# Softmax attention stage: full-width side products split into four strips of 32 output columns

## The chip, the cores and the metric

One program on one core of a Trainium2 chip. The metric is the device time of one execution in microseconds, as the median of several runs. Besides its time, one execution of the kernel was recorded by the hardware profiler; everything that is said of durations comes from that record.

## What is computed

The reference is a chain of six layers on `x` of shape (4, 1024, 128) in fp32. The part in which the change lies is the softmax attention, 16 heads of 8 channels, together with the second channel-mixing layer, which is computed beside it:

```python
x = x + 0.5 * _L0_ffn_ref(_layernorm(x), L0_ffn_W_r, L0_ffn_W_k, L0_ffn_W_v, L0_ffn_mu_r, L0_ffn_mu_k)
x = x + _L0_attn_ref(_layernorm(x), L0_attn_qkv_w, L0_attn_qkv_b, L0_attn_proj_w, L0_attn_proj_b)
x = x + 0.5 * _L0_ffn_ref(_layernorm(x), ...)        # the same weights a second time
x = x + 0.5 * _L1_ffn_ref(...)                       # 8 experts, top 2
x = x + _L1_attn_ref(...)                            # linear attention
x = x + 0.5 * _L1_ffn_ref(...)

def _L0_attn_ref(x, qkv_w, qkv_b, proj_w, proj_b):
    q, k, v = split_heads(x @ qkv_w.T + qkv_b)       # 16 heads of 8
    q, k = apply_rotary(q), apply_rotary(k)
    attn = softmax(q @ k^T * 8 ** -0.5)              # 1024 x 1024 for each head
    return (attn @ v) @ proj_w.T + proj_b

def _L0_ffn_ref(x, W_r, W_k, W_v, mu_r, mu_k):
    xr, xk = mix(x, x_prev, mu_r), mix(x, x_prev, mu_k)
    return sigmoid(xr @ W_r.T) * (relu(xk @ W_k.T) ** 2 @ W_v.T)
```

## The kernel before

The token axis is cut into 32 tiles of 128 tokens, four tiles make a group (512 tokens, one PSUM bank), two groups a batch. The program has stages that follow one another: a start (the first channel mixing of the first groups and the queries and keys of batch 0), the softmax attention, expert loops, the linear attention, expert loops again.

The attention stage is a list of 256 steps (`A_STEPS`: 4 batches, 2 halves of queries, 4 groups of four heads, 8 tiles of keys). TensorE runs, in program order and for each step n (function `pe_attention`):

- the scores (L986): four bf16 matmuls of 50 contracted rows by 128 output columns, moving 512 elements each, two at rows 0 to 49 and two at rows 64 to 113 of the array, into two of three pairs of PSUM banks. Each pair waits until the exponentials of three pairs earlier are done;
- the side pieces that a planner (`plan_attention`) put on this step: at most one of those that use TensorE;
- the weighted sums of step n - 2 (L1003): four fp32 matmuls, each with 128 contracted rows and 18 output columns and 512 moving elements. The four go to PSUM partitions 0, 32, 64 and 96, so each takes one strip of 32 array columns. They wait for the exponentials of their step.

An fp32 matmul stands as two records in the trace. So L986 has four records a step and L1003 eight. ScalarE runs two exponentials of 128x1024 for each step (L1275, `attn_probs<-ps`).

The side pieces are the rest of the work of this stage: the queries, keys and values of the next batch, the division and projection of the finished heads, and the second channel mixing, whose layer is spread over the stage. All of them go through one PSUM bank (`AUX`, bank 7), so a piece waits until VectorE or ScalarE has read out the one before it. Those that use TensorE are:

- `rot` (L890): a rotated or unrotated half of queries or keys, one fp32 product of 128x128 weights with 256 moving elements;
- `norms` (L900): one bf16 product with 512 moving elements;
- `val` (L912): the values, two fp32 products with 128 moving elements a piece;
- `proj` (L948): the projection, four fp32 products with 128 moving elements;
- `mk` (L769): one fp32 product with 512 moving elements; `mr` (L773) and `mv` (L779): four fp32 products with 128 moving elements each;
- transposes (L595, helper `pe_turn_group`), the router's products (L1457) and some small ones (L921, L930).

VectorE and GpSimd work for the same pieces: `dve_attention_side` and `dve_side_mix` take the products out of PSUM (L1099 for `rot`, L1129 for `norms`), split queries and keys into bf16 parts (L1106 to L1125), divide (L1152, L1156) and normalise (L584). Each engine takes the pieces of a step in the same order, which is written out in `k.a_plan`.

## Time and profile before

| | us |
|---|---|
| three runs, median (lowest to highest) | 1315.74 (1309.18 to 1320.01) |
| span of the profiled execution, first to last instruction | 1294.8 |
| difference of the median and the span | 20.9 |
| the attention stage within the span, first to last exponential | 84.0 to 647 |

The profiled execution has no time of its own beside its span, so the difference of 20.9 us between the median of the runs and the span stands for what lies around the span. In the trace, PE is TensorE's matmuls and PEld its weight loads, DVE is VectorE, ACT ScalarE, POOL GpSimd. A matmul's row gives its start and its full duration, which reaches beyond the start of the next one, since matmuls are pipelined: the pitch from start to start is what counts for the time. "idle before" is how long the engine had nothing to do before the instruction, and the arrow names what released it.

### The profile page before, as it was taken

What the parts mean: (1) busy time and instruction counts of PE and PEld (TensorE: products, weight loads), DVE (VectorE), ACT (ScalarE), POOL (GpSimd) and SP (SyncE); (2) the same over time, 40 slices, a digit from 0 to 9 for tenths busy, and PEclk for the clock granted to TensorE, in tenths of its full rate; (3) what the DMA queues carried; (4) which work ended last, traced back from release to release, by engine and by line L of the source; (5) the groups of instructions that cost most, each with busy time, mean ns of one, the idle gap of its engine ahead of it and who ended that gap; (6) DMA issues with size and microseconds to landing.
All of it is one profiled execution on the core that took longest, in us unless ns stands there. A gap on an engine that the chain in (4) does not pass through costs nothing. (4 is left out here: it accounts for less than half of the span.)

```text
span 1294.8 us, 21020 instructions
## 1 busy us (share of the span) xinstructions
PE 1070.8 (83%) x7616; PEld 500.4 (39%) x7616; DVE 653.5 (50%) x2099; ACT 807.3 (62%) x1164; POOL 373.6 (29%) x376
## 2 busy tenths in 40 slices
PE   4479998999999999999978858888877986998940
PEld 3242222322222231232256535534544554665620
DVE  5762555366356332333156326657867684633522
ACT  4348787877898989999934525555544441464520
POOL 2100110211110102333010664144331165265435
PEclk8679998999999999999998979989888897998975
DMA  5270370027028500300011323200000011233422
GB/s 144 55 105 1 58 101 2 1 41 106 14 42 120 157 1 15 114 17 18 19 38 49 104 83 94 68 17 20 15 14 5 1 34 58 72 109 110 133 66 67
DMA packets 83796, 74.08 MB, mean 57 GB/s; under 512 B 11440, under 2 KB 77872, under 8 KB 82800
## 3 DMA queue, kind: packets, MB, share of 16 engines
q1 hardware_dynamic: 73900, 54.93, 19.2%
q0 software_dynamic: 8192, 16.79, 4.4%
q8 instruction: 66, 1.08, 0.4%
q10 hardware_dynamic: 1604, 0.99, 0.3%
q14 instruction: 34, 0.28, 0.1%
HBM read 39.26 MB, written 33.42 MB: 56 GB/s over the span
## 5 line engine op out<-in xcount | busy, mean ns | idle before, releaser
L1275 ACT ACTIVATE attn_probs<-ps 128x1024 f32<-128x1024 f32 x512 | 485.5, 1072 | 73.1 <-PE ps L986 73.0
L1003 PE MATMUL ps<-attn_probs,attn_v 128*18 128x512 f32 x2048 | 274.9, 610 | 6.3 <-DVE room L1234 5.6
L1641 POOL DMA_INDIRECT slots<-moe_xr,moe_slot x128 | 124.8, 975 | 184.4 <-ACT attn_probs L1275 82.7
L986 PE MATMUL ps<-stack 50*128 50x512 bf16 x1024 | 166.2, 389 | 7.2 <-issue 1.2
L1651 POOL DMA_INDIRECT moe_back<-results,moe_slot x128 | 123.3, 963 | 115.2 <-PE ps L1696 45.4
L1706 PE MATMUL ps<-stack,lin_scores 128*128 x312 | 153.1, 613 | 0.0
L1807 ACT ACTIVATE lin_scores<-ps 128x256 f32<-128x256 f32 x156 | 58.5, 382 | 114.9 <-PE ps L1706 114.8
L986 PEld LDWEIGHTS ps<-stack 50*128 50x128 bf16 x1024 | 34.0, 94 | 244.1 <-ACT attn_probs L1275 229.3
L1780 DVE TENSOR_TENSOR lin_scores<-ps,lin_scores 128x256 f32<-128x256 f32 x156 | 59.1, 419 | 104.6 <-ACT lin_scores L1807 104.5
L1732 PE MATMUL ps<-stack,lin_scores 128*128 x624 | 85.1, 280 | 4.8 <-ACT lin_heads_out L1820 4.8
L1732 PEld LDWEIGHTS ps<-stack,lin_scores 128*128 128x128 f32 x624 | 77.4, 195 | 6.5 <-issue 6.5
L1706 PEld LDWEIGHTS ps<-stack,lin_scores 128*128 128x128 f32 x312 | 55.5, 199 | 39.5 <-issue 39.5
L1313 POOL TENSOR_TENSOR room<-room 128x512 f32<-128x512 f32 x16 | 22.2, 1387 | 165.2 <-DVE room L1099 165.2
L1003 PEld LDWEIGHTS ps<-attn_probs,attn_v 128*18 128x18 f32 x2048 | 34.8, 96 | 76.8 <-issue 52.8
L1773 DVE TENSOR_SCALAR lin_scores<-ps,c_norm_scale 128x256 f32<-128x256 f32 x80 | 37.9, 474 | 51.1 <-PE ps L1696 50.6
L1696 PE MATMUL ps<-c_ident,moe_gathered 128*128 128x128 f32 x156 | 33.1, 294 | 36.2 <-DMA moe_gathered<-slots 28.7
L2138 DVE TENSOR_TENSOR lin_scores<-ps,c_causal 128x512 f32<-128x512 f32 x64 | 41.1, 683 | 37.1 <-PE ps L2009 37.1
L2208 ACT ACTIVATE lin_scores<-ps 128x512 f32<-128x512 f32 x64 | 34.7, 594 | 37.4 <-PE ps L2009 37.4
L1099 DVE SCALAR_TENSOR_TENSOR room<-ps,c_attn_b,moe_xr 128x512 f32<-128x512 f32 x32 | 23.9, 749 | 65.3 <-PE ps L890 63.8
L1718 PEld LDWEIGHTS ps<-c_ident,lin_scores 128*128 128x128 f32 x312 | 39.0, 143 | 37.4 <-issue 35.0
L1813 ACT ACTIVATE lin_scores<-ps 128x512 f32<-128x512 f32 x80 | 46.7, 584 | 10.1 <-PE ps L1718 7.2
L552 DVE BATCH_NORM_STATS2 stats<-x 128x6 f32<-128x128 f32 x192 | 41.5, 279 | 19.9 <-POOL x L864 8.3
(237 smaller groups left out, 1552.1 us busy)
## 6 DMA issues: line engine op xcount, KB each, us to landing
moe_gathered<-slots SPq DMA_DIRECT2D x76, 128.0 KB, 2.3
results<-lin_heads_out SPq DMA_DIRECT2D x76, 128.0 KB
stack<-qk_parts SPq DMA_DIRECT2D x36, 256.0 KB, 8.9
slots<-zeros SPq DMA_DIRECT2D x2, 2496.0 KB, 15.2
qk_parts<-moe_xr SPq DMA_DIRECT2D x32, 128.0 KB, 2.7
qk_parts<-moe_xr SPq DMA_DIRECT2D x16, 192.0 KB, 2.8
stack<-in_expert_w SPq DMA_DIRECT2D x1, 3072.0 KB, 10.4
stack<-qk_parts SPq DMA_DIRECT2D x12, 192.0 KB, 10.6
```

The source lines that it names most:

```text
L552: instruction = V.bn_stats(out=k.stats[:, t, :], in_=k.x[:, t, :])
L986: instruction = T.matmul(k.ps[:, SCORE_BANKS[i % 3][s], :], d.stack[b % 2][rows, 1, pair, kt * P:(kt + 1) * P], d.stack[b % 2][rows, 0, pa ...
L1003: instruction = T.matmul(k.ps[32 * j:32 * j + STRIP, PV_BANK, :], d.v[:, b % 2, kt, first:first + STRIP], d.probs[:, n % A_PROBS, j * BANK ...
L1275: A.activation(d.probs[:, n % A_PROBS, 2 * e * BANK:2 * (e + 1) * BANK], k.ps[:, banks[0]:banks[1] + 1, :].rearrange("p a n -> p (a n)"), ...
L1641: G.indirect_dma_start(out=k.dram["slots"][half], out_offset=bass.IndirectOffsetOnAxis(ap=d.slot[:, s, at, c:c + 1], axis=0), in_=d.xr[:, ...
L1651: G.indirect_dma_start(out=k.back[:, at % RING, c, :], out_offset=None, in_=k.dram["results"][half], in_offset=bass.IndirectOffsetOnAxis(a ...
L1706: T.matmul(k.ps[:, bank, :], d.gt[:, u % NB, i, :], w[:, bass.ds(offset[u, i], 2 * HIDDEN)], start=True, stop=True).then_inc(k.full[bank], 1)
L1732: instruction = T.matmul(k.ps[:, bank, i * DIM:(i + 1) * DIM], d.ht[:, u % NB, i, c * P:(c + 1) * P], w[:, 2 * HIDDEN + c * DIM:][:, bass. ...
L1780: V.tensor_tensor(d.h[:, u % NB, i, :], k.ps[:, bank, 0:HIDDEN], d.silu[:, u % NB, i, :], ALU.mult).then_inc(k.free[bank], 1)
L1807: A.activation(d.silu[:, u % NB, i, :], k.ps[:, bank, HIDDEN:2 * HIDDEN], ACT_FN.Silu).then_inc(k.e_silu, 1)
L1813: A.activation(d.ht[:, u % NB, 0:width, :].rearrange("p i c -> p (i c)"), k.ps[:, bank, 0:width * HIDDEN], ACT_FN.Copy).then_inc(k.free[ba ...
L2138: V.tensor_tensor(d.scores[:, m % NS, :].rearrange("p (j t) -> p j t", j=HPG), k.ps[:, bank, :].rearrange("p (j t) -> p j t", j=HPG), caus ...
```

## The change

A helper `pe_product` writes one product of 128x128 weights as several matmuls, each with a share of the output columns. With `strips=4` it makes four matmuls of 32 output columns, at PSUM partitions 0, 32, 64 and 96, each with the whole contraction of 128 rows and the same moving operand. With `strips=1` it makes the matmul of before. Only the attention stage passes `HPG`, which is 4; the start and the expert loops keep one strip. Transposes, L1457, L921 and L930 stay as they are. The semaphore is raised by the last strip.

```diff
+def pe_product(T, out, weights, moving, strips):
+
+    width = P // strips
+    for j in range(strips):
+        cols = slice(width * j, width * (j + 1))
+        instruction = T.matmul(out[cols, :], weights[:, cols], moving, start=True, stop=True)
+    return instruction
+
+
-def pe_side_mix(T, k):
+def pe_side_mix(T, k, strips=1):
...
-            T.matmul(k.ps[:, bank, :], w[:, 1, :], d.mixed_k, start=True, stop=True).then_inc(k.full[bank], 1)
+            pe_product(T, k.ps[:, bank, :], w[:, 1, :], d.mixed_k, strips).then_inc(k.full[bank], 1)
...
-                instruction = T.matmul(k.ps[:, bank, i * P:(i + 1) * P], d.mixed_r[:, i * P:(i + 1) * P], w[:, 0, :],
-                                       start=True, stop=True)
+                instruction = pe_product(T, k.ps[:, bank, i * P:(i + 1) * P], d.mixed_r[:, i * P:(i + 1) * P], w[:, 0, :], strips)
...
-            instruction = T.matmul(k.ps[:, bank, cols], w[:, 2 * qk + which, :],
-                                   d.xt[:, half * BANK:(half + 1) * BANK][:, cols], start=True, stop=True)
+            instruction = pe_product(T, k.ps[:, bank, cols], w[:, 2 * qk + which, :],
+                                     d.xt[:, half * BANK:(half + 1) * BANK][:, cols], strips)
...
 def pe_attention(T, k):
     d = k.attn
-    side = pe_attention_side(T, k)
+    side = pe_attention_side(T, k, HPG)
...
-    mix, route = pe_side_mix(T, k), pe_route(T, k)
+    mix, route = pe_side_mix(T, k, HPG), pe_route(T, k)
```

`mv`, `norms`, `val` and `proj` are edited in the same way. Counted in the programs, the pieces that the change reaches in the attention stage are 48 `rot`, 12 `norms`, 12 `val`, 7 `proj` and 11 each of `mk`, `mr` and `mv`: 112 in all. The order of VectorE, ScalarE, GpSimd and the DMA queues is the same before and after.

TensorE's order around a `rot` piece, in the middle of batch 0's steps, before (`room` holds the transposed input, `c_qk_w` the weights; 128x256 is the output):

```order
L986 MATMUL ps<-stack 128x512 x4
L890 MATMUL ps<-room,c_qk_w 128x256
L1003 MATMUL ps<-attn_probs,attn_v 18x512 x4
L986 MATMUL ps<-stack 128x512 x4
L900 MATMUL ps<-room,same_head_bf 128x512
```

and after:

```order
L993 MATMUL ps<-stack 128x512 x4
L756 MATMUL ps<-room,c_qk_w 32x256 x4
L1010 MATMUL ps<-attn_probs,attn_v 18x512 x4
L993 MATMUL ps<-stack 128x512 x4
L756 MATMUL ps<-room,same_head_bf 32x512 x4
```

Nothing changes its place; the one matmul has become four of 32 output columns (all at the helper's line, L756), still between the scores and the weighted sums.

The same around the products of four tiles, `mr` and `proj`, some 15 steps later, before:

```order
L773 MATMUL ps<-c_mix_w,mix_mixed_r 128x128 x4
L1003 MATMUL ps<-attn_probs,attn_v 18x512 x4
L986 MATMUL ps<-stack 128x512 x4
L595 MATMUL ps<-c_ident,room 128x128 x4
...
L948 MATMUL ps<-c_attn_vo,room 128x128 x4
L1003 MATMUL ps<-attn_probs,attn_v 18x512 x4
```

and after:

```order
L756 MATMUL ps<-c_mix_w,mix_mixed_r 32x128 x16
L1010 MATMUL ps<-attn_probs,attn_v 18x512 x4
L993 MATMUL ps<-stack 128x512 x4
L595 MATMUL ps<-c_ident,room 128x128 x4
...
L756 MATMUL ps<-c_attn_vo,room 32x128 x16
L1010 MATMUL ps<-attn_probs,attn_v 18x512 x4
```

Four matmuls have become sixteen, that is eight records sixteen times two; the transposes (L595) are as before.

## Rows read from the trace of the kernel before

**Rows 1.** Windows of the attention stage, exponentials (L1275) alone: window, length, busy (count), clock

```profile
84.00:470.00 386.00, 319.62 (x334) 0.96 0.32 56
470.00:647.00 177.00, 165.86 (x179) 1.00 0.10 34
```

**Rows 2.** Waits in the attention stage: who for whom, us in total, times, longest

```profile
ACT attn_probs L1275 <- PE ps L986: 73.0, 136, 5.3
```

**Rows 3.** Timeline of PE, two steps without a side piece: start, duration, what

```profile
519.71 0.92 PE L986 MATMUL ps<-stack 50*128 50x512 bf16 x4
...
521.54 0.92 PE L986 MATMUL ps<-stack 50*128 50x512 bf16 x4
```

**Rows 4.** Timeline of PE, steps with a `rot` piece

```profile
344.77 0.60 PE L986 MATMUL ps<-stack 50*128 50x512 bf16 x4
345.30 0.70 PE L890 MATMUL ps<-room,c_qk_w 128*128 128x256 f32 x2
345.93 1.05 PE L1003 MATMUL ps<-attn_probs,attn_v 128*18 128x512 f32 x8
346.92 0.60 PE L986 MATMUL ps<-stack 50*128 50x512 bf16 x4
```

**Rows 5.** Timeline of PE, steps with `mk` and `mr`

```profile
609.84 1.13 PE L769 MATMUL ps<-room,c_mix_w 128*128 128x512 f32 x2
610.89 1.05 PE L1003 MATMUL ps<-attn_probs,attn_v 128*18 128x512 f32 x8
...
612.41 1.16 PE L773 MATMUL ps<-c_mix_w,mix_mixed_r 128*128 128x128 f32 x8
613.50 1.05 PE L1003 MATMUL ps<-attn_probs,attn_v 128*18 128x512 f32 x8
```

**Rows 6.** Timeline of PE, end of the stage: weighted sums of two steps running on

```profile
644.59 1.91 PE L1003 MATMUL ps<-attn_probs,attn_v 128*18 128x512 f32 x16
```

**Rows 7.** Timeline of PE, linear attention: short strips running on

```profile
1073.16 0.84 PE L2022 MATMUL ps<-lin_scores,lin_v 128*9 128x128 f32 x24
1073.82 0.25 PE L1952 MATMUL ps<-lin_v,lin_k_tok 128*32 128x36 f32 x8
```

**Rows 8.** Groups of PE by line and shape, attention stage: records, busy, mean ns, idle before

```profile
L890 PE MATMUL ps<-room,c_qk_w 128*128 128x256 f32 x96 | 34.3, 440 | 4.7 <-DVE attn_heads_out L1156 4.2 <-DVE attn_longest L1129 0.5
L773 PE MATMUL ps<-c_mix_w,mix_mixed_r 128*128 128x128 f32 x88 | 13.7, 302 | 1.4 <-DVE attn_longest L1129 1.4
L779 PE MATMUL ps<-c_mix_w,moe_gathered 128*128 128x128 f32 x88 | 12.7, 288 | 0.0
L769 PE MATMUL ps<-room,c_mix_w 128*128 128x512 f32 x22 | 12.4, 645 | 0.0
L912 PE MATMUL ps<-c_attn_vo,room 128*128 128x128 f32 x48 | 8.5, 300 | 0.0
L948 PE MATMUL ps<-c_attn_vo,room 128*128 128x128 f32 x56 | 8.1, 288 | 0.0
L900 PE MATMUL ps<-room,same_head_bf 128*128 128x512 bf16 x12 | 4.7, 389 | 1.2 <-DVE moe_gathered L817 1.2
```

**Rows 9.** Timeline of PE around a wait for VectorE

```profile
134.44 0.70 PE L890 MATMUL ps<-room,c_qk_w 128*128 128x256 f32 x2 [2.10 <-DVE attn_heads_out L1156]
135.07 1.92 PE L1003 MATMUL ps<-attn_probs,attn_v 128*18 128x512 f32 x8
136.92 1.03 PE L986 MATMUL ps<-stack 50*128 50x512 bf16 x4
```

**Rows 10.** Timeline of PE, a `norms` piece and what stands around it

```profile
366.23 0.60 PE L986 MATMUL ps<-stack 50*128 50x512 bf16 x4
366.77 0.39 PE L900 MATMUL ps<-room,same_head_bf 128*128 128x512 bf16 x1
...
368.07 0.60 PE L986 MATMUL ps<-stack 50*128 50x512 bf16 x4
```

**Rows 11.** Groups of PE over the whole span: L2022

```profile
L2022 PE MATMUL ps<-lin_scores,lin_v 128*9 128x128 f32 x1024 | 46.9, 287 | 0.0
```

More of the change, by code:

```diff
@@ L778, in side @@
             for i in range(TPG):
-                instruction = T.matmul(k.ps[:, bank, i * P:(i + 1) * P], side_areas(k, j)[1][:, i * P:(i + 1) * P], w[:, 2, :],
-                                       start=True, stop=True)
+                instruction = pe_product(T, k.ps[:, bank, i * P:(i + 1) * P], side_areas(k, j)[1][:, i * P:(i + 1) * P], w[:, 2, :],
+                                         strips)
             instruction.then_inc(k.full[bank], 1)
@@ L866, in pool_side_mix, with pe_attention_side @@
     return side
-def pe_attention_side(T, k):
+def pe_attention_side(T, k, strips=1):
     d, w = k.attn, k.const["qk_w"]
@@ L899, in side @@
             T.wait_ge(k.a_square, 4 * b + i + 1)
-            T.matmul(k.ps[:, bank, :], k.same_head[:, :], d.square[:, i % 2, :], start=True,
-                     stop=True).then_inc(k.full[bank], 1)
+            pe_product(T, k.ps[:, bank, :], k.same_head[:, :], d.square[:, i % 2, :], strips).then_inc(k.full[bank], 1)
         elif kind == "val":
@@ L911, in side @@
                 at = half * BANK + i * P
-                instruction = T.matmul(k.ps[:, bank, i * P:(i + 1) * P], d.xt[:, at:at + P],
-                                       k.const["attn_vo"][:, 0, :], start=True, stop=True)
+                instruction = pe_product(T, k.ps[:, bank, i * P:(i + 1) * P], d.xt[:, at:at + P], k.const["attn_vo"][:, 0, :],
+                                         strips)
             if part:
@@ L947, in side @@
             for i in range(TPG):
-                instruction = T.matmul(k.ps[:, bank, i * P:(i + 1) * P], d.proj_in[:, i * P:(i + 1) * P],
-                                       k.const["attn_vo"][:, 1, :], start=True, stop=True)
+                instruction = pe_product(T, k.ps[:, bank, i * P:(i + 1) * P], d.proj_in[:, i * P:(i + 1) * P],
+                                         k.const["attn_vo"][:, 1, :], strips)
             instruction.then_inc(k.full[bank], 1)
```

## The prediction

> **What bounds the kernel now.** I read the stage by windows first, then the waits of ScalarE, and then TensorE's timeline step by step. In [rows 1] the reader sees two stretches of the attention stage. In the first, 386 us long, the exponentials are busy for 319.6 us and so idle for 66; in the second, 177 us long, they are idle for 11. The waits say for whom: 73.0 us of that idleness ended with the scores L986, in 136 waits [rows 2]. So ScalarE sets the pace of this stage in some steps and TensorE in others.
>
> Which steps those are is seen in the timeline. A step without a side piece repeats after 521.54 - 519.71 = 1.83 us [rows 3]. That is two exponentials at ScalarE's own pace, and the floor of a step. A step with a `rot` piece repeats after 346.92 - 344.77 = 2.15 us, and its parts fill it without a gap: 0.53 from the scores to the piece, 0.63 from the piece to the weighted sums, 0.99 from these to the next scores [rows 4]. TensorE is the bound there, by 0.32 us a step. With a `mk` piece, 1.05 us stand in place of the 0.63, and with `mr` 1.09 [rows 5]; the latter makes a step of 0.53 + 1.09 + 0.99 = 2.61 us. A `norms` piece fits: its step takes 368.07 - 366.23 = 1.84 us, which is the floor [rows 10].
>
> **What the change removes.** All 112 pieces that it reaches stand between scores and weighted sums, as in [rows 4, 5, 10]. The streamed elements stay the same: four strips side by side read the moving operand at the same time, as the weighted sums do. Two things go. The first is the load of a full 128-column weight tile ahead of the piece's first matmul, which nothing hides because the array changes over from the scores. The second is the change-over from a full-width product to strips ahead of the weighted sums. The price of both is read from places where strips follow strips.
>
> At the end of the stage the weighted sums of two steps run on: 16 records last 1.91 us [rows 6], and eight last 1.05 [rows 4]. Eight more records of 512 elements thus cost 0.86 us behind their like, while eight by themselves take 0.99 to the next group; 0.13 us of this is change-over. For short strips, the 24 records of 128 elements of L2022 take 1073.82 - 1073.16 = 0.66 us, so four strips side by side cost 0.11 [rows 7]. From this, piece and weighted sums together:
> - `rot`: before 0.63 + 0.99 = 1.62. After, eight records of 256 elements, half of 0.86 = 0.43, and 0.99: 1.42. Saved 0.20.
> - `mk`: before 1.05 + 0.99 = 2.04. After 0.86 + 0.99 = 1.85. Saved 0.19.
> - `mr`, `mv`, `proj`: before 1.09 + 0.99 = 2.08. After, 32 records in eight rounds of four, 8 x 0.11 = 0.88, and 0.99: 1.87. Saved 0.21.
> - `val`, two such products: its before and after lie near those of `rot`; I take 0.20.
> - `norms`: its step is at the floor already, so 0 whatever TensorE saves.
>
> The counts are the groups' records divided by those of a piece: 96/2 = 48 `rot`, 22/2 = 11 `mk`, 88/8 = 11 each of `mr` and `mv`, 56/8 = 7 `proj`, 48/4 = 12 `val` [rows 8]. That gives 48 x 0.20 + 12 x 0.20 + 11 x 0.19 + 29 x 0.21 = 20.2 us of TensorE's time.
>
> **What of it shows.** The step with `rot` becomes 0.53 + 0.43 + 0.99 = 1.95 us, still above the floor of 1.83, so the 0.20 is visible in full; the steps with four products stay above it by more (2.40). Some pieces stand behind steps in which TensorE had run ahead and are covered already. The program has these 100 pieces and, beside them, 51 of transposes and of the router, all longer than the floor allows, against 136 waits of ScalarE for TensorE [rows 2]. So about a tenth is covered, and I take a tenth of 20.2 off, 2.0 us.
>
> More goes to VectorE. Where TensorE waits for it, an earlier arrival lengthens the wait, and the one or two pieces just ahead save nothing. The waits of the changed lines add up to 4.7, 1.4 and 1.2 us [rows 8], in five places, and I put those of the transposes and small products, which the chosen rows leave out, at some fifteen more. If half of these twenty places swallow 0.35 us each, that is 3.5 us. The bounds are 0 (VectorE's work shifts along with the products that feed it) and 8 (every place swallows two pieces' saving, 20 x 0.4).
>
> The weights of a strip are 32 columns wide here, against 18 and 9 in the strips that I read. The one group with 32 columns, L1952, runs on behind L2022 with eight records in 0.25 us, tail included [rows 7]. So a load of this width can cost a piece some hundredths at most; with 0.03 on 100 pieces, 3 us at the worst and 0 at best. I take 0, since loads of later strips lie behind matmuls.
>
> Nothing is added on another engine, and no wait is added. After the stage the expert loops start from the last division and projection, so they shift along.
>
> Sum: 20.2 - 2.0 - 3.5 = 14.7 us. Against the profiled execution's span of 1294.8 this gives 1280.1; the median of the runs lies 20.9 above the span, which the change leaves alone, so 1280.1 + 20.9 = 1301.0 us.
>
> **Rivals.**
> 1. *VectorE takes back half.* The queries of three batches hold twelve splits of VectorE, and the mixing has eleven chains from product to product. If each of these 23 swallows 0.3 us (6.9) in place of my 3.5, and two more waits end with the clock down, the gain shrinks. Such a fall is seen in [rows 9]: after a wait of 2.10 us the weighted sums last 1.92 instead of 1.05, and take 136.92 - 135.07 = 1.85 us to the scores instead of 0.99, at the lower of the clock's two levels (1.2 instead of 2.4 GHz). It costs 0.9 us there and some more in the scores behind, say 1.5 together. The gain is then 20.2 - 2.0 - 6.9 - 3.0 = 8.3, the time 1307.4. For it: the granted clock of 0.96 in the first stretch shows that such falls happen [rows 1]. Against it: the long runs of `rot` steps like [rows 4] have no wait for VectorE at all.
> 2. *Issue becomes the bound* (the side of slower). The 29 pieces of four products have 32 matmul records in place of 8, and `val` 16 in place of 4. If a record costs r, their sum is (29 x 32 + 12 x 16) r = 1120 r, against 29 x 1.09 + 12 x 0.63 = 39.2 us before; the other 59 pieces still save 11.8. The change loses from r = 51.0 / 1120 = 0.046 us on. L2022 shows 0.66 / 24 = 0.028 us where it runs on [rows 7], which four strips' streaming explains, and 46.9 / 1024 = 0.046 us on average, gaps and tails within [rows 11]. If wider strips took double the former, 0.055, the kernel would be 1120 x 0.055 - 51.0 = 10.6 us slower: 1326. The row that runs on speaks against it, though its 24 records are fewer than 32.
> 3. *The strips do not share the array*, because they read the same moving operand, so that the change doesn't do what it says. Then `rot` streams 4 x 0.43 = 1.72 us and the long pieces some 3.5: 60 x 1.1 + 40 x 2.4 = 162 us more, 1478. The weighted sums speak against it: eight records of 512 elements in strips last 1.05 us together [rows 4], as long as the two full-width ones of `mk`, 1.13 [rows 5]. But their strips read different operands.
> 4. *Nothing is lost to VectorE* and the falls of the clock get fewer: 20.2 - 2.0 + 2 = 20.2 us, 1295.5 (the 2 for one or two falls less, at 1.5 each, as above).
>
> On rival 2 the Trainium skill, "TensorE: Matmul & The Clock Gate", section "Wait — 56ns, not 53.3ns?", states a floor of about 25 ns from matmul to matmul however small they are, and 62 ns where the sequencer decodes them in firmware. By the first nothing changes, since the streaming asks for as much; by the second r would be 0.062 and the time 1334 (estimate from the page's figure). The trace sides with the first: the 0.028 us per record of [rows 7] lie below 62 ns.
>
> **How the numbers follow.** Forecast (gain of 10 to 19, 1297 to 1306) 0.57; rival 1 0.27; rival 2 0.08; rival 3 0.02; rival 4 0.06. A measurement of this kernel can tell about 1%, 13.2 us, from no change. Of the forecast's chance some four fifths lie beyond 13.2 us of gain (0.46), of rival 1 next to none but a little for noise in the medians (0.05), and rival 4 does (0.06): faster 0.57. Slower by over 1%: most of rival 2 (0.05) and rival 3: 0.07. The rest, 0.36, is within 1%. The range is 1290 to 1317: rival 4 with some luck of the medians (the three runs span 11 us) below, rival 1 and a neutral rival 2 above.
>
> **What would show it.** In the changed kernel's timeline, the `rot` steps should repeat after 1.95 us, with 0.43 to 0.46 from the first strip to the weighted sums; `mr` to the weighted sums 0.88 to 0.92; ScalarE's idle time ahead of the exponentials should fall from 73 to about 58 us, and the stage should end about 15 us earlier. The records of four strips should start within hundredths of a microsecond. Wrong would be a pitch of short strips above 0.11 for four (rival 2), starts of strips one behind another (rival 3), or TensorE's waits for VectorE grown by over 6 us and more windows below full clock (rival 1).

## The result, and the profile after

| | before | changed | ratio (95% interval) |
|---|---|---|---|
| median of four runs, us | 1316.82 (1309.18 to 1320.01) | 1298.69 (1291.63 to 1304.51) | 0.987 (0.984 to 0.990) |
| span of the profiled execution, us | 1294.8 | 1298.4 | |
| first to last start of an exponential, us | 561.5 (84.0 to 645.6) | 546.5 (83.7 to 630.2) | |
| what follows the last exponential, us | 649.2 | 668.1 | |

The forecast was 1301.0, a gain of 14.7 us; measured are 18.1, and the interval of the ratio spans 13.6 to 21.2. The two profiled spans do not show this gain: the changed kernel's is even 3.6 us longer. The stage that was changed is 15.0 us shorter there, and the rest of the program, in which no instruction differs, is 18.9 us longer. The first experiment takes up that contradiction.

All exponentials of the changed kernel: least, median and longest duration in ns, then the first and the last start in us:

```profile
L1282 ACT ACTIVATE attn_probs<-ps x512: 1012/1026/1582, 83.7 to 630.2; 128x1024 f32<-128x1024 f32 x171
```

Windows of the stage, exponentials alone, in the columns of [rows 1]:

```profile
84.00:470.00 386.00, 334.37 (x351) 0.97 0.32 56
470.00:632.00 162.00, 149.90 (x162) 0.97 0.10 37
```

In the first stretch, of the same length as before, 351 exponentials stand in place of 334. The second stretch is now 162 us long, but its granted clock is 0.97 where [rows 1] had 1.00: something new is slow there.

Waits in the stage, as in [rows 2]:

```profile
ACT attn_probs L1282 <- PE ps L993: 57.8, 74, 5.3
```

ScalarE's idle time fell from 73.0 to 57.8 us, and the view has 74 waits where it had 136. Most of the others are not gone but shorter than the 0.15 us from which the view counts a wait: a `rot` step still takes 1.97 us (below), more than ScalarE's 1.83.

TensorE's timeline around a `rot` piece, the answer to [rows 4]:

```profile
341.22 0.61 PE L993 MATMUL ps<-stack 50*128 50x512 bf16 x4
341.76 0.64 PE L756 MATMUL ps<-room,c_qk_w 128*32 128x256 f32 x8
342.21 1.04 PE L1010 MATMUL ps<-attn_probs,attn_v 128*18 128x512 f32 x8
343.19 0.60 PE L993 MATMUL ps<-stack 50*128 50x512 bf16 x4
```

The piece leads to the weighted sums in 0.45 us instead of 0.63, and the step repeats after 1.97 us instead of 2.15. The duration of the piece's row, 0.64, is barely shorter than the 0.70 of before; only the pitch shows the gain.

The same for `mv` and then `mk`, beside [rows 5]:

```profile
539.02 1.08 PE L756 MATMUL ps<-c_mix_w,moe_gathered 128*32 128x128 f32 x32
539.92 1.04 PE L1010 MATMUL ps<-attn_probs,attn_v 128*18 128x512 f32 x8
540.89 0.61 PE L993 MATMUL ps<-stack 50*128 50x512 bf16 x4
541.43 1.06 PE L756 MATMUL ps<-room,c_mix_w 128*32 128x512 f32 x8
542.31 1.04 PE L1010 MATMUL ps<-attn_probs,attn_v 128*18 128x512 f32 x8
```

Four tiles lead to the sums in 0.90 us instead of 1.09, with 32 records in place of 8; `mk` in 0.88 instead of 1.05. The weighted sums themselves still take 0.97 to 0.99.

A `norms` piece, the answer to [rows 10], is shorter as well:

```profile
351.19 0.61 PE L993 MATMUL ps<-stack 50*128 50x512 bf16 x4
351.73 0.40 PE L756 MATMUL ps<-room,same_head_bf 128*32 128x512 bf16 x4
...
352.92 0.61 PE L993 MATMUL ps<-stack 50*128 50x512 bf16 x4
```

TensorE's `norms` step repeats after 1.73 us instead of 1.84. ScalarE's own step is 1.82 there (1.84 before), but the `rot` step behind it is 1.87 for ScalarE and not 1.97: what TensorE gains at the piece shows one step later.

The groups of the changed line in the stage, as in [rows 8]:

```profile
L756 PE MATMUL ps<-room,c_qk_w 128*32 128x256 f32 x384 | 30.7, 391 | 4.9 <-DVE attn_heads_out L1163 4.2 <-DVE attn_longest L1136 0.7
L756 PE MATMUL ps<-c_mix_w,mix_mixed_r 128*32 128x128 f32 x352 | 12.0, 278 | 1.6 <-DVE attn_longest L1136 1.6
L756 PE MATMUL ps<-c_mix_w,moe_gathered 128*32 128x128 f32 x352 | 11.9, 276 | 1.3 <-ACT moe_xrt L845 0.8 <-DVE attn_longest L1136 0.4
```

The waits of the changed lines grew little: 4.7 to 4.9 for `rot`, 1.4 to 1.6 for `mr`, and 1.3 new ones for `mv`, of which 0.8 are for ScalarE, which has to read out the piece before. Over all lines, TensorE's waits for VectorE in the stage add up to 24.4 us before and 27.6 after.

The slow place of the second stretch, in the changed kernel's timeline of PE. In brackets stands the idle time before the row and what ended it:

```profile
554.55 0.92 PE L993 MATMUL ps<-stack 50*128 50x512 bf16 x4
556.98 0.66 PE L595 MATMUL ps<-c_ident,moe_xr 128*128 128x128 f32 x4 [1.51 <-DVE moe_xr L1510]
557.56 1.68 PE L1010 MATMUL ps<-attn_probs,attn_v 128*18 128x512 f32 x8
559.18 1.04 PE L993 MATMUL ps<-stack 50*128 50x512 bf16 x4
560.15 1.87 PE L1464 MATMUL ps<-router_scaled,moe_xrt 128*128 128x8 f32 x8
561.95 1.91 PE L1010 MATMUL ps<-attn_probs,attn_v 128*18 128x512 f32 x8
```

The same steps in the kernel before:

```profile
576.15 0.66 PE L595 MATMUL ps<-c_ident,moe_xr 128*128 128x128 f32 x4 [1.05 <-DVE moe_xr L1503]
576.73 1.05 PE L1003 MATMUL ps<-attn_probs,attn_v 128*18 128x512 f32 x8
...
578.25 1.06 PE L1457 MATMUL ps<-router_scaled,moe_xrt 128*128 128x8 f32 x8
579.24 1.05 PE L1003 MATMUL ps<-attn_probs,attn_v 128*18 128x512 f32 x8
```

Because TensorE arrives earlier, it waits 1.51 us for VectorE's normalised router input instead of 1.05. Then its clock falls to the lower level (1.2 instead of 2.4 GHz): the sums last 1.68 and 1.91 us where they had lasted 1.05. Counted from a step's first exponential to the next step's, the steps 220 to 222 take 4.05 + 4.61 + 3.84 = 12.5 us against 2.75 + 2.51 + 2.30 = 7.6, a loss of 4.9 us.

### The profile page after: what moved, and what is told of

It reads as the page before. It is cut to its first block, busy times and chain, and to the rows that moved or that the text cites. A ratio compares the mean times of both kernels' runs of the same rounds, so it can differ in the third digit from the quotient of the medians.

```text
span 1298.4 us, 23480 instructions
## 1 busy us (share of the span) xinstructions
PE 1065.0 (82%) x8846; PEld 502.6 (39%) x8846; DVE 653.2 (50%) x2099; ACT 805.7 (62%) x1164; POOL 374.6 (29%) x376
## 4 chain that ended last, share of the span: by engine, by line
PE 54%; DVE 20%; ACT 11%; issue 5%; POOL 3%; DMA 1%; another core or an unknown queue 1%; ACTq 0%; POOLq 0%; SPq 0%; DVEq 0%
PE ps L1010 10%; PE ps L1713 9%; ACT attn_probs L1282 9%; PE ps L993 6%; PE ps L756 6%; PE ps L1739 4%; PE ps L595 3%; PE ps L2016 2%; POOL moe_back L1658 2%; PE ps L1725 2%; DVE lin_scores L2145 2%; PE ps L2029 2%; DVE stats L552 1%; PE ps L1703 1%; PE ps L1940 1%
## 5 line engine op out<-in xcount | busy, mean ns | idle before, releaser
L1282 ACT ACTIVATE attn_probs<-ps 128x1024 f32<-128x1024 f32 x512 | 484.6, 1075 | 59.3 <-PE ps L993 57.8
L1713 PE MATMUL ps<-stack,lin_scores 128*128 x312 | 154.3, 618 | 0.0
L1739 PE MATMUL ps<-stack,lin_scores 128*128 x624 | 86.5, 283 | 8.8 <-ACT lin_heads_out L1827 6.8
L1010 PEld LDWEIGHTS ps<-attn_probs,attn_v 128*18 128x18 f32 x2048 | 45.6, 97 | 61.5 <-issue 41.9
L1320 POOL TENSOR_TENSOR room<-room 128x512 f32<-128x512 f32 x16 | 22.3, 1392 | 153.6 <-DVE room L1106 153.6
L1703 PE MATMUL ps<-c_ident,moe_gathered 128*128 128x128 f32 x156 | 33.4, 296 | 30.4 <-DMA moe_gathered<-slots 18.9
L1827 ACT ACTIVATE lin_heads_out<-ps 128x256 f32<-128x256 f32 x80 | 30.2, 378 | 34.2 <-PE ps L1739 23.8
```

Of the source, the lines that this page charges most:

```text
L1010: instruction = T.matmul(k.ps[32 * j:32 * j + STRIP, PV_BANK, :], d.v[:, b % 2, kt, first:first + STRIP], d.probs[:, n % A_PROBS, j * BANK ...
L1282: A.activation(d.probs[:, n % A_PROBS, 2 * e * BANK:2 * (e + 1) * BANK], k.ps[:, banks[0]:banks[1] + 1, :].rearrange("p a n -> p (a n)"), ...
L1713: T.matmul(k.ps[:, bank, :], d.gt[:, u % NB, i, :], w[:, bass.ds(offset[u, i], 2 * HIDDEN)], start=True, stop=True).then_inc(k.full[bank], 1)
L1739: instruction = T.matmul(k.ps[:, bank, i * DIM:(i + 1) * DIM], d.ht[:, u % NB, i, c * P:(c + 1) * P], w[:, 2 * HIDDEN + c * DIM:][:, bass. ...
```

## The experiments

Times are medians, and ratios are to the kernel before on the same chip. "Stage" is the time from the first to the last start of an exponential in the profiled execution.

### The kernel before, once more

No edit.

> The kernel before, unchanged, profiled a second time. The question is the span: the first profile of before has a span of 1294.8 us and an attention stage of 561.6 us (first to last exponential), yet the runs' median is 1316.8; the profile after has 1298.4 and 546.5. Theory: the stage's gain of 15 us is the change's, and the 19 us by which the rest of the span is longer after than before is a profile of before that happened to be quick behind the stage. Then this profile has a stage of 560 to 563 us and a span of 1307 to 1318. Rival: strips in the attention stage cost something behind it (code loading, transfers that collide). Then this profile repeats the span of 1295 within 3 us.

Measured: 1319.2 against 1319.2, ratio 1.001 (0.998 to 1.003). Exponentials of this profiled execution:

```profile
L1275 ACT ACTIVATE attn_probs<-ps x512: 1015/1023/1619, 85.3 to 646.6; 128x1024 f32<-128x1024 f32 x171
```

The stage takes 561.3 us, as in the profile of before, and 670.0 follow instead of 649.2. Both are as the theory had it, and the rival, a cost of the strips behind their stage, falls: the kernel before shows the longer rest too. Its span is 1316.6 and its run 1318.5, so 1.9 us lie around the span, and for the changed kernel 1300.2 - 1298.4 = 1.8. The 20.9 us of the prediction were no time around the span: the profiled execution of before, at 1294.8, was quicker than each of its timed runs, of which the lowest is 1309.18.

Where it was quick is seen in the linear attention stage, whose records of the short strips (L2022 before, L2029 after) run from 851.6 to 1080.7 in the profile of before, 229.1 us. Of the later runs in which that stage was unchanged, those on one chip took 229 there too, but for one execution with 234, and those on two others, like the changed kernel's first execution, 245 to 247. The changed kernel shows this with no edit at all between its two executions. First its row from the first execution, then from its second, on the quick chip:

```profile
L2029 PE MATMUL ps<-lin_scores,lin_v x1024: 269/273/421, 840.9 to 1085.7; 128*9 128x128 f32 x171
```

```profile
L2029 PE MATMUL ps<-lin_scores,lin_v x1024: 272/273/421, 843.4 to 1072.4; 128*9 128x128 f32 x171
```

That is 244.8 against 229.0 us, 15.8 of the 17.0 us by which these two executions differ in what follows the last exponential (668.1 against 651.1). Its place can be given more closely: for the first 201 us of this stretch the records of the two executions stand at the same distances, and the rest takes 43.8 us (1041.9 to 1085.7) against 28.0 (1044.4 to 1072.4). In that rest the granted clock is 0.82 against 1.00, and TensorE stands idle 6.8 us against 0.6 in waits for which the profile names no engine. What sets this off no run shows. The chip of the two first executions, the profile of before among them, is not on record; that they fit the one group of chips and the other is all that speaks for the chip as the cause. So a stage is to be compared with itself, and whole times only on one chip.

### Only `rot` in strips

```diff
-            pe_product(T, k.ps[:, bank, :], k.same_head[:, :], d.square[:, i % 2, :], strips).then_inc(k.full[bank], 1)
+            pe_product(T, k.ps[:, bank, :], k.same_head[:, :], d.square[:, i % 2, :], 1).then_inc(k.full[bank], 1)
...
-    mix, route = pe_side_mix(T, k, HPG), pe_route(T, k)
+    mix, route = pe_side_mix(T, k), pe_route(T, k)
```

`val` and `proj` likewise get one strip.

> Strips for the 48 query and key pieces alone (L890 of before), all other side products full width. Theory (each piece saves its own exposed weight load and one change-over, and the savings add up): rot steps repeat after 1.97 us as in the changed kernel, against 2.15; 48 x 0.185 = 8.9 us less what is covered, so the stage is 7 to 10 us shorter than 561.6, and the time 0.5 to 0.8% under before. Rival (VectorE is what bounds the query phases, and the shorter steps return as longer waits): the stage is less than 4 us shorter although the steps without a wait show 1.97.

Measured: 1308.06, ratio 0.994 (0.992 to 0.997). The `rot` step takes 1.97 us as in the changed kernel, and the stage 549.3 us (82.4 to 631.6), 12.2 less than in the profile of before. Of this, 8.9 us are the `rot` pieces, 48 times 0.185. Another 4.4 come from places where the clock no longer falls, at steps 20, 21, 84 and 98, and waits are 1.2 longer. The rival, under 4 us, is refuted; the clock's part may differ in another execution, as the changed kernel's second one below shows.

### All but `rot` in strips

```diff
             instruction = pe_product(T, k.ps[:, bank, cols], w[:, 2 * qk + which, :],
-                                     d.xt[:, half * BANK:(half + 1) * BANK][:, cols], strips)
+                                     d.xt[:, half * BANK:(half + 1) * BANK][:, cols], 1)
```

> The complement: strips for norms, val, proj, mk, mr and mv, the query and key pieces full width. Theory: val steps 1.97 against 2.16, mk 2.39 against 2.58, four-tile products 2.41 against 2.61, norms at the floor; 52 pieces x 0.195 = 10 us less a tenth, the stage 6 to 9 us shorter than 561.6; with the other half (e2) the two sum to the 15 us of the whole change within 4 us, which is what one or two falls of the clock more or less are worth. Rival (the parts are not additive, since one hides the other's waits): the sum is off by more than 5 us.

Measured: 1313.31, ratio 0.996 (0.994 to 0.998). The stage takes 554.3 us (83.5 to 637.8), 7.2 less. The steps are those of the changed kernel: 1.97 with `val`, 2.39 with `mk`, 2.41 with four tiles. A new fall of the clock stands at steps 160 to 162. There this kernel's timeline reads:

```profile
443.64 0.65 PE L595 MATMUL ps<-c_ident,moe_xr 128*128 128x128 f32 x4 [1.41 <-DVE moe_xr L1510]
444.22 1.75 PE L1010 MATMUL ps<-attn_probs,attn_v 128*18 128x512 f32 x8
```

These steps last 4.02 + 4.61 + 3.77 us against 2.94 + 2.51 + 2.30 in the kernel before, 4.65 us more, behind a wait of 1.41 instead of 1.25 us. The changed kernel waits 1.41 us there as well, and its sums keep their 1.05. By medians the two halves of the change give 11.1 and 5.9 us, together 17.0 beside the 18.1 of the whole. By stages they give 12.2 and 7.2, together 19.4 beside 15.0: off by 4.4, more than the 4 that were allowed for and less than the 5 of the rival. The pieces themselves add up, 8.9 + 11.6 = 20.5 us in TensorE's steps, which is what the whole change takes from them; the difference lies in the clock, which gave 4.4 us back in the first half and took 0.6 in this one and 1.3 in the whole.

### Two strips of 64 columns

```diff
-    side = pe_attention_side(T, k, HPG)
+    side = pe_attention_side(T, k, 2)
...
-    mix, route = pe_side_mix(T, k, HPG), pe_route(T, k)
+    mix, route = pe_side_mix(T, k, 2), pe_route(T, k)
```

> The changed kernel with two strips of 64 output columns in place of four of 32. Theory (a saving of 0.19 us is made of two: the load ahead of the first matmul, exposed in proportion to its columns, and the change-over ahead of the weighted sums, which goes only if the piece has the same strips of 32 as these): with 64 columns half of the load is left and the change-over stays, so the rot step repeats after 2.09 to 2.11 us (2.15 full width, 1.97 with four strips) and a third of the gain is left, the stage 3 to 7 us shorter than 561.6. Rival (the gain is that strips of any width need no change-over): 1.99 to 2.03 and a stage 12 to 15 us shorter.

Measured: 1314.42, ratio 0.997 (0.995 to 0.999); the stage is 6.4 us shorter. Timeline of PE around a `rot` piece in this kernel:

```profile
341.16 0.60 PE L993 MATMUL ps<-stack 50*128 50x512 bf16 x4
341.70 0.65 PE L756 MATMUL ps<-room,c_qk_w 128*64 128x256 f32 x4
342.28 1.05 PE L1010 MATMUL ps<-attn_probs,attn_v 128*18 128x512 f32 x8
343.27 0.60 PE L993 MATMUL ps<-stack 50*128 50x512 bf16 x4
```

The piece leads to the sums in 0.58 us, between 0.63 and 0.45, and the step takes 2.11. So half as wide strips save 0.05. If that is the load, and its time goes with its width, four strips save 0.075 by it, and the other 0.11 of their 0.185 is the change-over to the sums' mode of the array, which two strips do not avoid. [rows 6] had given 0.13 for that. This division rests on the proportion and was not measured by itself.

The Trainium skill, "TensorEngine Tiling (Array Packing)", section "Key Properties", says that a change of the tiling mode drains TensorE, and gives no time. The runs fit it: some 0.11 us here, by this division.

### The changed kernel, once more

No edit; on the quick chip, with the next three.

> The changed kernel, unchanged, profiled a second time, for how much of its stage is chance. Theory (the steps without a wait are fixed, the falls of TensorE's clock after waits for VectorE are not): rot steps again 1.97 us and four-tile steps 2.41, the rest of the span behind the last exponential again 665 to 673 us, and the stage within 541 to 552 us (546.5 before this), the difference made by where the weighted sums run at the lower clock (6.5 steps in the first profile). Rival: the falls belong to the kernel, so the stage repeats within 1 us and the slow place at 556 to 568 us with it.

Measured: 1285.24 against 1297.71, ratio 0.991 (0.988 to 0.993). That is 12.5 us (8.7 to 15.8 by the interval) for the same edit that had given 18.1. The stage takes 550.4 us (85.4 to 635.7), 3.8 more than in the changed kernel's first execution, at the same steady steps. What follows the last exponential takes 651.1, outside the 665 to 673 expected. The slow place repeats:

```profile
562.77 0.66 PE L595 MATMUL ps<-c_ident,moe_xr 128*128 128x128 f32 x4 [1.50 <-DVE moe_xr L1510]
563.35 1.56 PE L1010 MATMUL ps<-attn_probs,attn_v 128*18 128x512 f32 x8
```

It belongs to the kernel. Three other falls, at steps 20, 51 and 84, stand in this execution and not, or only in part, in the first: those are spread. The one at step 20 stands behind the same wait as in [rows 9]:

```profile
133.87 1.08 PE L756 MATMUL ps<-room,c_qk_w 128*32 128x256 f32 x8 [2.10 <-DVE attn_heads_out L1163]
134.72 1.93 PE L1010 MATMUL ps<-attn_probs,attn_v 128*18 128x512 f32 x8
```

### The router's product in strips too

```diff
-                instruction = T.matmul(k.ps[:, bank, i * EXPERTS:(i + 1) * EXPERTS], d.xrt[:, g % 2, i * P:(i + 1) * P],
-                                       k.router[:, :], start=True, stop=True)
+                instruction = pe_product(T, k.ps[:, bank, i * EXPERTS:(i + 1) * EXPERTS], d.xrt[:, g % 2, i * P:(i + 1) * P],
+                                         k.router[:, :], strips)
```

It has 128 weight columns and only 8 moving elements, so the issue of records (rival 2 of the prediction) would show here first.

> The changed kernel with the attention stage's six router products in four strips as well (128x8 outputs, four tiles a piece: 32 records of 8 moving elements in place of 8). Nothing is streamed to speak of, so this shows what a record and a 32-column weight load cost. Theory (loads of four strips run side by side, the piece now takes 0.99 us because eight full loads of 0.12 follow one another): piece to weighted sums 0.25 to 0.4 us, the six steps of 2.5 to 2.65 us fall to 1.83 to 1.9, the stage 3 to 5 us shorter than the changed kernel's. Rival (issue bounds many small records, at the 0.028 us a record that the streaming strips show): 32 x 0.028 = 0.9 us and no gain; above 0.046 a record, a piece of 1.5 us and steps of 3 us.

Measured: 1275.96, ratio 0.984 (0.980 to 0.988). The stage takes 538.4 us (83.0 to 621.4). Timeline of PE, steps with the router's pieces in this kernel:

```profile
434.60 0.66 PE L595 MATMUL ps<-c_ident,moe_xr 128*128 128x128 f32 x4 [1.40 <-DVE moe_xr L1510]
435.19 1.05 PE L1010 MATMUL ps<-attn_probs,attn_v 128*18 128x512 f32 x8
...
436.71 0.44 PE L756 MATMUL ps<-router_scaled,moe_xrt 128*32 128x8 f32 x32
436.98 1.05 PE L1010 MATMUL ps<-attn_probs,attn_v 128*18 128x512 f32 x8
```

Thirty-two records take 0.27 us to the next group, 8.4 ns each, where eight full-width ones had taken 0.99. Issue is no bound, and the loads of the four strips run side by side: one of them lasts 114 ns on average in the trace, and the records follow at 8.4. A product that is nearly all weight load becomes 3.7 times as quick. Six such pieces stand in the stage; from 2.51 us to the floor of 1.83 that is 4.1 us, within the 3 to 5 expected. The stage is 12.0 us shorter than the changed kernel's on this chip, and the other 8 us, which were not expected, lie at the clock: 5.5 steps have their sums at the lower level instead of 9.6. Three of them are the spread named above, and the slow place has one step at that level where it had two in full and part of a third, though its wait is 1.50 us as before.

By the Trainium skill, "TensorE: Matmul & The Clock Gate", section "Wait — 56ns, not 53.3ns?", no matmul starts less than about 25 ns behind the one before. By that the piece would take 32 x 25 = 800 ns (estimate from the page's figure). The trace shows 270, and the measurement decides.

### Strips in the linear attention as well

The router's edit, and in the linear attention's side products (L1940 to L1989 of the changed kernel):

```diff
-                T.matmul(k.ps[:, bank, 0:HEADS * VW], d.q[:, gg % NQ, c * P:(c + 1) * P],
-                         d.state[:, u % NST, :, :].rearrange("p h c -> p (h c)"), start=True,
-                         stop=False).then_inc(k.l_inter, 1)
+                pe_product(T, k.ps[:, bank, 0:HEADS * VW], d.q[:, gg % NQ, c * P:(c + 1) * P],
+                           d.state[:, u % NST, :, :].rearrange("p h c -> p (h c)"), strips, True, False).then_inc(k.l_inter, 1)
...
-                instruction = T.matmul(k.ps[:, bank, gr * HPG * VW:(gr + 1) * HPG * VW],
-                                       d.sums[:, u % 2, gr * P:(gr + 1) * P], k.const["head_rows"][:, :],
-                                       start=first, stop=first or gr == HEAD_GROUPS - 1)
+                instruction = pe_product(T, k.ps[:, bank, gr * HPG * VW:(gr + 1) * HPG * VW],
+                                         d.sums[:, u % 2, gr * P:(gr + 1) * P], k.const["head_rows"][:, :], strips,
+                                         first, first or gr == HEAD_GROUPS - 1)
```

The queries, keys, values and projection there are edited likewise.

> As e6, and the same strips for the linear attention's products between its scores and its weighted sums: 32 pieces of sums over head rows (128x36, four a piece, 0.8 to 1.0 us now), 28 state products (128x144), 14 + 7 + 8 of 512 or four times 128 columns, and the router's twelve. Theory: TensorE is busy through this stage, so 32 x 0.55 (loads side by side) + 57 x 0.15 + 12 x 0.6 = 33 us of its time go, of which half is covered by VectorE and ScalarE; the kernel is 10 to 25 us faster than the changed one. Rival (the linear stage is bound by the chain from scores over VectorE and ScalarE to the sums): less than 5 us.

Measured: 1263.19, ratio 0.975 (0.972 to 0.978). Timeline of PE in this kernel, state and head sums:

```profile
878.62 0.45 PE L756 MATMUL ps<-lin_state,stack 128*32 128x144 f32 x8
878.89 0.48 PE L756 MATMUL ps<-c_head_rows,lin_sums 128*32 128x36 f32 x32
879.22 0.62 PE L2027 MATMUL ps<-lin_scores,lin_v 128*9 128x128 f32 x16
```

and in the kernel before:

```profile
906.26 0.51 PE L1964 MATMUL ps<-lin_state,stack 128*128 128x144 f32 x2
906.61 0.98 PE L1969 MATMUL ps<-c_head_rows,lin_sums 128*128 128x36 f32 x8
907.52 0.62 PE L2022 MATMUL ps<-lin_scores,lin_v 128*9 128x128 f32 x16
```

The head sums (36 moving elements) take 0.33 us instead of 0.91. There are 32 of them, so 18.6 us; the linear stage's short strips run from 826.0 to 1038.9, 212.9 us, against 229.0 in the two executions on this chip that had that stage as before, 16.1 less (the kernel with the router's strips alone took 234.4, though its edit does not reach this stage). The medians of the two kernels differ by 12.8.

### Turns of rest ahead of the waits

A helper lets the planner leave TensorE's side slot empty for some steps, so that VectorE has its result ready when TensorE comes:

```diff
+def wait_after(pieces, kind, steps):
+
+    out = []
+    for piece in pieces:
+        out.append(piece)
+        if piece[1][0] == kind:
+            out += [(OTHER, ("rest",))] * steps
+            kind = None
+    return out
...
-            begin.setdefault(n + 1, []).append(list(route_part(1, 0, TPB)))
+            begin.setdefault(n + 1, []).append(wait_after(route_part(1, 0, TPB), "rnorm", 2))
```

and likewise behind the norms, the mixing's normalisation and the first router part; `VALUES_AT` goes from 7 to 10 and `FIRST_AT` for batch 3 from 48 to 50.

> The changed kernel with empty turns in the planner ahead of the transposes that wait for a long piece of work on VectorE (4 turns behind the first normalisation, 2 behind later ones and behind the router's, 5 in the third batch's mixing, which begins 2 steps later); nothing else is changed, every engine does the same work. It tests what is left of the stage's excess over the floor. Theory (some 35 us of it lie in steps in which TensorE stands behind a wait for VectorE and then runs at the lower clock): steps over 2.75 us fall from 17 to under 8, weighted sums at the lower clock from 6.5 steps to under 3, and the stage is 10 to 20 us shorter than 546.5. Rival (VectorE's work has to be waited for sooner or later, the waits only move to other pieces): less than 4 us.

Measured: 1285.53, ratio 0.990 (0.987 to 0.993): the changed kernel's own 1285.24 on this chip. The stage takes 549.7 us. The rival holds: 19 steps over 2.75 us where under 8 were expected, 5.5 steps of sums at the lower clock where under 3. The slow place has shrunk (2.77 + 3.61 + 2.59 us in its three steps, one of them still with sums at the lower clock, 1.91 us), but the waits have moved. One of the new ones, in this kernel's timeline of PE:

```profile
383.18 1.39 PE L768 MATMUL ps<-c_attn_vo,room 128*32 128x128 f32 x32 [1.95 <-DVE room L1181]
384.27 2.01 PE L1022 MATMUL ps<-attn_probs,attn_v 128*18 128x512 f32 x8
```

The projection waits 1.95 us for a division that now stands behind other work of VectorE, and the clock falls there instead.

### Rest at the slow place alone

Only the two turns behind the last router part's normalisation, that is the last hunk above.

> The changed kernel with two empty turns between the normalisation and the transposes of the router's part in the last batch, and nowhere else. There the changed kernel's TensorE arrives 0.45 us earlier at the transposes, waits 1.51 us for VectorE in place of 1.05, and then runs three steps at half clock (4.05 + 4.61 + 3.84 us, against 2.75 + 2.51 + 2.30 before), in two profiles of two. Theory (the length of that wait decides): with the transposes a step or two later the wait is under 1 us, the granted clock stays at full through the place, and the stage is 4 to 6 us shorter than in a profile of the changed kernel with as many falls elsewhere, 541 to 546 us. Rival (the fall comes from what TensorE did earlier, and would come wherever the router stands): the three steps stay above 10 us together.

Measured: 1299.15 against 1321.43, ratio 0.984 (0.980 to 0.988). The changed kernel was not timed on this chip, so the ratio is no measure of the turns beside its own 0.987 and 0.991; the stage is. It takes 542.4 us (85.7 to 628.1), within the 541 to 546 expected. The same place in this kernel:

```profile
561.30 0.66 PE L606 MATMUL ps<-c_ident,moe_xr 128*128 128x128 f32 x4
561.89 1.05 PE L1021 MATMUL ps<-attn_probs,attn_v 128*18 128x512 f32 x8
...
564.31 1.03 PE L1475 MATMUL ps<-router_scaled,moe_xrt 128*128 128x8 f32 x8 [0.83 <-ACT moe_xrt L1624]
565.27 1.05 PE L1021 MATMUL ps<-attn_probs,attn_v 128*18 128x512 f32 x8
```

No wait stands ahead of the transposes, and the sums keep their 1.05 us. The steps from 218 up to 226 take 17.2 us instead of 22.3: 5.0 us, the size of the 4.9 that the changed kernel lost there. That removing the wait removes the fall is shown here; that it always does is not, for in the version with rest everywhere these steps are arranged alike, TensorE has the same wait of 0.83 us, and one step of sums behind it ran at the lower clock.

### Both together

The linear attention's strips, the router's, and the two turns of rest.

> All that gained: the changed kernel, strips for the router and the linear attention's products (e7), and the two empty turns of e9. If the gains add up: e7's ratio to before of 0.975 less 2.5 to 5 us of 1298, so 0.971 to 0.974; the stage 533 to 537 us. Rival: since e7's router pieces are short, its fall there costs only 2 us (4.40 + 2.09 + 2.30), and the turns bring less than 1 us: 0.974 to 0.976.

Measured: 1287.46, ratio 0.976 (0.972 to 0.979), stage 536.8 us. The ratio equals that of the version without the turns (0.975), but the two stand on different chips, and what the turns are worth can't be read from it: with the same program there, the short strips of the linear stage run 239.2 us here and 212.9 in the version without the turns. By the attention stage the turns give 1.6 us (538.4 to 536.8): the clock takes 3.5 us less, 1.7 of them at the slow place, where the router's strips had already cut the fall short, and waits are 2.1 longer. The version with strips in both attentions is 1.7% quicker than the changed kernel on the same chip (1263.19 against 1285.24).

## Why the prediction was right, and where not

The gain and its sign are as forecast, and so is its place: ScalarE's waits for TensorE in steps whose TensorE work exceeds the floor.

- **Saved by a piece.** `rot` 0.18 to 0.185 against 0.20, `mk` 0.19 against 0.19, four tiles 0.20 against 0.21, `val` 0.19 against 0.20. With the counts: 48 x 0.185 + 12 x 0.19 + 11 x 0.19 + 29 x 0.20 = 19.1 us against 20.2. The price of strips read from "strips behind strips" was good to 0.02 us; a `rot` of 256 elements takes 0.45, not 0.43. `norms` was put at nothing "whatever TensorE saves", and that was wrong: the 1.84 of its step were TensorE's own parts without a gap, 0.53 + 0.32 + 0.99, and ScalarE's 1.83 is no floor of a single step. Where TensorE is behind, a step without a piece repeats after 1.52 (372.38 to 373.90 in the kernel before). TensorE saves 0.12 at each of the twelve, 1.4 us, and so 20.5 in all.
- **What is covered.** In TensorE's steps the stage is 15.0 us shorter (560.2 to 545.2), so 5.5 of the 20.5 us did not arrive, and 2.0 + 3.5 = 5.5 were forecast. The sum is right by luck, its terms are not. A tenth covered behind steps in which TensorE had run ahead: the trace shows nothing of it, for the 85 steps without a piece take the same time before and after within 0.2 us altogether, and TensorE's waits for the exponentials did not grow (6.5 and 6.4 us, short ones included). That tenth had been worked out from 136 waits against 151 long steps, from a view that leaves out short waits. Waits for VectorE: 3.2 us longer against 3.5. The other waits, most of all those until ScalarE has read out the piece before, are 1.0 longer, and the clock took 1.3; both had been left out of the sum.
- **The clock.** It stood only in the rivals, and both directions happened. In the first execution the falls at steps 20, 21 and 84 vanished (5.41 + 2.63 to 4.13 + 1.97 us, and 5.77 to 4.10), and at 220 to 222 one came (4.9 us lost). Taken over all steps with slow sums, what goes beyond their steady length and their idle time is 11.4 us before (11.2 in its second execution) and 12.7 after (16.8 in its second, where the falls at 20 and 84 were back). So in these two executions the change costs clock, 1.3 and 5.6 us, and rival 4, which had it gain, did not come about.
- **VectorE takes back half** (rival 1) did not happen: TensorE's waits for VectorE grew by 3.2 us, half of the over 6 that were its sign. Its fall behind a longer wait did, for one place instead of two, and at 4.9 us instead of the 1.5 that I had read from [rows 9], since three steps ran at the lower clock there and not one.
- **Issue as the bound** (rival 2) is refuted by the router's product, 8.4 ns a record against the 46 from which the change would lose. **Strips that do not share the array** (rival 3) are refuted by every step above: four tiles in 0.90 us.
- **The wrong step** is "the median lies 20.9 above the span, which the change leaves alone". The difference lies mostly in the linear attention stage, where other executions on another chip show it too, and 1.8 us lie around a span. It did no harm, since 1315.74 - 14.7 gives the forecast all the same; whoever had compared the spans of the two profiles would have found a change that loses 3.6 us. The profile's own table could have raised the doubt: a span 14.4 us below the lowest of three runs is not what lies around it.

How large the gain is, the runs say only roughly: the edit gave 18.1 us in the first measurement and 12.5 on the quick chip, and in the stage 15.0 and, against the same profile of before, 11.2. The forecast of 14.7 lies between.

What remains open: what lets the clock fall. A wait of 1.51 us (and 1.50, 1.41) was followed by the lower clock, one of 1.05 and one of 1.25 were not; but the version with the router's strips waits 1.40 us at its first router part and keeps its clock, the changed kernel waits 1.41 there, as the kernel that lost it did, and keeps it too, and the changed kernel keeps it behind this wait, the answer to [rows 9]:

```profile
131.78 0.64 PE L756 MATMUL ps<-room,c_qk_w 128*32 128x256 f32 x8 [2.10 <-DVE attn_heads_out L1163]
132.24 1.04 PE L1010 MATMUL ps<-attn_probs,attn_v 128*18 128x512 f32 x8
```

The same wait of 2.10 us was followed by sums of 1.92 us in the kernel before, and by sums of 1.93 in the second execution of this very kernel. The length of the wait alone does not decide. Why the end of the linear stage is some 16 us longer on two of the three chips, at a lower granted clock, is open too.

## What to carry to other kernels

Where full-width fp32 products stand between products that occupy strips of columns, writing them as four strips of 32 columns saves 0.2 us a piece here (a change-over and a part of the weight load, as far as two strips tell them apart), and most where few elements move for many weights (0.99 to 0.27 us). Before a piece is put at nothing because its step "is at the floor", check whether the engine's own parts fill that step. When an engine gets quicker, look for the next wait behind which the clock may fall, and give only that place a turn of rest; rest everywhere moved the waits and gained nothing. Compare stages within a trace, and whole times only on one chip.

## What the runs showed of the hardware that was not expected

- Matmul records of four column strips follow one another at 8.4 ns on average, loads included (32 in 0.27 us).
- The program takes 1.7% to 1.8% more time on two of the chips (1319.2 and 1321.4 against 1297.7 for the kernel before). Some 16 to 18 us of it lie in the last part of one stage, the linear attention, where the granted clock is 0.82 to 0.85 on these, and 1.00 in two of three executions on the other.
- A wait for VectorE that grew by 0.46 us, to 1.51, cost the three steps around it 4.9 us, nearly all of it through the clock.
